# One hybrid block on one core: the end of a chunk taken in single pieces, one per tile, and another order around the tiles

## The chip, the cores and the metric

The kernel runs on one core of one Trainium2 chip. TensorE is called PE here (its weight loads PEld), VectorE DVE, ScalarE ACT, GpSimd POOL, SyncE SP. The metric is the device time of one execution in microseconds (us). A multiplication on PE shows as MATMUL rows; a float32 matmul shows as two rows.

## The reference, cut to what matters

Two sequences of 2048 tokens with 256 features go through four residual parts, each behind a layer norm:

```python
x = x + attn_a(layernorm(x))   # softmax attention, 16 heads, 4 key/value heads
x = x + ffn(layernorm(x))      # three cycles of: tf = sigmoid(net(out)); out = out + coupling * twist(out)
x = x + attn_b(layernorm(x))   # linear attention, causal, no softmax:
#   q, k = rope(silu(y@Wq)), rope(silu(y@Wk)); v = y@Wv
#   out = tril(q k^T) v;  out = layernorm(out * sigmoid(y@Wg1@Wg2)) * ln_w + ln_b;  out @ Wo
x = x + ffn(layernorm(x))      # the same coupling net again
```

## The kernel before, in words

The 4096 tokens lie as 8 chunks of 512 tokens (`NCH`), or 32 tiles of 128 tokens (`TILES`), four tiles to a chunk. `X` holds the residual stream by token, `YT` the normed and transposed stream that the matmuls read. Every engine has its own instruction stream, written out by hand; engines wait for each other by counting semaphores. There are four stages in time: softmax attention, first feed-forward (`feed_forward(0)`), linear attention in tiles (`through_tiles`), second feed-forward (`feed_forward(1)`).

**The tiles.** `through_tiles` calls each engine's `pipeline(n, ...)` for n = 0 to 33. In step n PE computes, in this order: `energy` of tile n (scores, L973), `rows` of tile n-1 (transpose back, L1008), `project_vg` of tile n+1 (L953), `project_qk` of tile n+2 (L944), `turn` of tile n+1 (L961), `attend` of tile n (L987, then L993 once all four masks are there, L999), on some tiles `turn_chunk` (L614), `out_proj` of tile n-2 (L1026), and `norm_turn` of tile n-1 (L1016). DVE computes four masks of tile n (L1734), among them the gated rows of tile n-1 (`gated`, L1755) and their statistics (L1758), then the variance, the rope of tile n+2 (L1718, L1727, L1728), `state` (L1747) and `residual` of tile n-2 (L1773). `project_qk` of tile n+2 writes the PSUM bank that `gated` of tile n-1 reads, so PE holds it until `gated` is done: `wait(pe, l_r, n - 2)`.

**The end of a chunk.** The last cycle of the first feed-forward is not finished before the tiles begin: for chunks 2 to 7 it is done between tiles. For each of these chunks there are seven pieces: `turned_rows` (ACT, L1148), `turned_minus` (DVE, L1599), `joined` (DVE, L1612, writes `X`), `moments_of` (DVE, four statistics L1416 and four aggregates L1423), `root` (POOL, L1838 to L1847), `spread` (ACT, L1140, makes the normed rows), and `turn_chunk` on PE with `put_rows` on ACT (L614, L1071, writes `YT`). On POOL `columns(n)` then copies tile n out of `YT` (L1960) for `project_qk` and `project_vg`. The table `MOMENTS_AT` sets the tile: chunk c has its moments in tile 3c-4, `turned_minus` and `joined` one tile ahead, `spread` one behind, rows two behind.

**The first tail.** The last steps of `feed_forward(0)` (`first`, `second`, `third`, `fourth`, `coupled` on ACT and PE, `update` on DVE) are written out one by one, with the first projections of the tiles among them: `queries_keys` (silu of q and k, L1334), `turned` (L1349 to L1355), `values_gate` (L1342, L1345). Silu and gelu lie in different ACT tables; a change of table is an ACT_TABLE_LOAD.

**The end of the tiles.** For the second feed-forward (stage 3) the moments of chunks 0 to 5 are made in steps 30 to 33, `spread(3, 0)` in step 31, and PE starts `first(0)` of `feed_forward(1)` (L830) once the last `residual` is done.

Of the kernel before, what the change touches and what calls it, by code (L numbers as in the profile page):

```python
# [63 lines left out]
MOMENTS_AT = {-1: 1, **{3 * c - 4: c for c in range(2, NCH)}}  # L64
# [6 lines left out]
def hybrid_block(nc, x, wq, bq, wk, bk, wv, bv, wo, bo, lq, lk, lv, lo, g1, g2, ln_w, ln_b,  # L71
                 c1, d1, c2, d2, c3, d3, c4, d4, e1, f1, e2, f2, e3, f3, ar,
                 ident_in, cos_in, sin_in, causal_in, head_in, diag_in, sign_in, out):
    with ExitStack() as ctx:
# [526 lines left out]
        def _(pe):  # L601
# [179 lines left out]
            def feed_forward(k):  # L781
# [113 lines left out]
                if k == 0:  # L895
# [18 lines left out]
                    project_qk(1, 1)  # L914
# [3 lines left out]
                    pe.wait_ge(n_y, 2 * (2 * NCH + 1))  # L918
                    project_vg(0, 0)
# [109 lines left out]
            def pipeline(n, p, place):  # L1029
# [15 lines left out]
                if n - 2 in MOMENTS_AT:  # L1045
                    turn_chunk(2, MOMENTS_AT[n - 2])
# [4 lines left out]
                if n - 2 in MOMENTS_AT:  # L1051
                    pe.wait_ge(n_y, 2 * (2 * NCH + MOMENTS_AT[n - 2] + 1))

# [12 lines left out]
        def _(act):  # L1066
# [85 lines left out]
            def feed_forward(k):  # L1152
# [71 lines left out]
                for n in range(LAST):  # L1224
# [3 lines left out]
                    if k == 1 and n + 2 < NCH:  # L1228
                        spread(st, n + 2)
# [18 lines left out]
                if k == 0:  # L1248
# [16 lines left out]
                    fourth(LAST - 1)  # L1265
                    first(LAST + 4)
                    second(LAST + 3)
                    coupled(LAST + 5)
                    third(LAST + 1)
                    turned_rows(k, 1)  # L1270
                    second(LAST + 4)
                    fourth(LAST + 1)
                    first(LAST + 5)
                    third(LAST + 3)
                    coupled(LAST + 6)
                    second(LAST + 5)
                    put_rows(2, 0)
                    fourth(LAST + 3)
                    first(LAST + 6)
# [3 lines left out]
                    queries_keys(1, 1)  # L1283
# [3 lines left out]
                    turned(0, 0)  # L1287
                    act.wait_ge(l_vz, 1)
# [77 lines left out]
            def pipeline(n, p, place):  # L1366
# [10 lines left out]
                if n - 2 in MOMENTS_AT:  # L1377
                    put_rows(2, MOMENTS_AT[n - 2])
                if n == TILES - 1:
                    spread(3, 0)  # L1380
                if n == TILES:
                    spread(3, 1)
                    put_rows(3, 0)
                if is_tile(n - 1):
                    affine(n - 1, 1 - p)
                if n - 1 in MOMENTS_AT:
                    spread(2, MOMENTS_AT[n - 1])
                if n + 2 in MOMENTS_AT:
                    turned_rows(0, MOMENTS_AT[n + 2])
                if n == TILES + 1:  # L1390
                    put_rows(3, 1)
# [9 lines left out]
        def _(dve):  # L1401
# [9 lines left out]
            def moments_of(st, c):  # L1411

                g = st * NCH + c
                wait(dve, n_mv, g - 1)
# [621 lines left out]
```

## Time and profile before

| | us |
|---|---|
| median of 3 runs (2078.86 to 2079.82) | 2079.09 |
| the profiled execution, its own time | 2074.16 |
| its span, first to last instruction | 2072.3 |
| PE busy | 1970.2 (95%) |
| DVE busy | 1807.6 (87%) |
| ACT busy | 1493.8 (72%) |
| POOL busy | 199.5 (10%) |

The granted clock of PE is 0.976 of full over the span. A busy share is an average over four stages with different limits; a stage is read by its windows and its timeline. "Idle before, and who ended it" stands in square brackets at the end of a timeline row. Rows of one instruction that follow each other are merged (x4), and the length is from the start of the first to the end of the last.

### The profile page before, as it was taken

To read this page: it belongs to the slowest core of one execution; us is meant where nothing else is said; L and a number is where in the kernel's file an instruction comes from. 1 tells how busy PE (TensorE), PEld (TensorE's weight loads), DVE (VectorE), ACT (ScalarE), POOL (GpSimd) and SP (SyncE) were. 2 spreads that over 40 slices of the span, in tenths; PEclk is the share of its full clock that TensorE was granted. 3 is DMA by queue.
4 is the path that set the end of the run, shared out by engine and by line. 5 is a ranking of instruction groups with operands and counts; after the bars stand their busy time and mean duration, and the time that the engine had idled before them with its cause. 6 is when DMAs were issued, how large, how long until landed. Compare 5 with 4: busy or idle time off the path is not lost.

```text
span 2072.3 us, 47390 instructions
## 1 busy us (share of the span) xinstructions
PE 1970.2 (95%) x14758; PEld 791.0 (38%) x14758; DVE 1807.6 (87%) x3350; ACT 1493.8 (72%) x2955; POOL 199.5 (10%) x442
## 2 busy tenths in 40 slices
PE   7899999999999999999999999989897889998995
PEld 4323333333333333333333333334433555665432
DVE  7899999999999999999999999955447788877358
ACT  5358888888888888888888888855546655545757
POOL 2300000000000000000000000041013111112012
PEclk9879999999999999999999999999999999999998
DMA  5431211221221122122112112122000000000002
GB/s 160 124 101 50 72 55 43 67 62 43 56 72 46 46 71 56 43 65 65 43 51 72 50 44 70 49 92 88 1 1 1 2 2 2 2 2 2 1 1 82
DMA packets 110205, 101.25 MB, mean 49 GB/s; under 512 B 52240, under 2 KB 91424, under 8 KB 110096
## 3 DMA queue, kind: packets, MB, share of 16 engines
q1 hardware_dynamic: 110096, 99.92, 17.7%
q8 instruction: 53, 0.87, 0.2%
q14 instruction: 56, 0.46, 0.1%
HBM read 78.79 MB, written 20.77 MB: 48 GB/s over the span
## 4 chain that ended last, share of the span: by engine, by line
PE 85%; DVE 8%; ACT 4%; issue 2%; DMA 1%; POOL 0%; SPq 0%; ACTq 0%; DVEq 0%; POOLq 0%
PE ps L694 24%; PE ps L669 16%; PE ps L717 11%; PE ps L723 11%; PE ps L830 5%; PE ps L839 3%; PE ps L944 3%; PE ps L953 2%; PE ps L683 2%; PE ps L1026 1%; PE ps L635 1%; PE ps L614 1%; PE ps L993 1%; DVE mx L1514 1%; PE ps L973 1%
## 5 line engine op out<-in xcount | busy, mean ns | idle before, releaser
L1514 DVE TENSOR_REDUCE mx<-ps 128x1 f32<-128x512 f32 x2048 | 1272.8, 682 | 10.8 <-PE ps L669 5.5
L1123 ACT ACTIVATE YT<-ps 128x512 f32<-128x512 f32 x2048 | 1056.5, 603 | 254.6 <-PE ps L723 254.6
L694 PE MATMUL ps<-YT,work 128*32 128x512 f32 x4096 | 546.1, 605 | 0.0
L669 PE MATMUL ps<-work 64*128 64x512 bf16 x2048 | 455.3, 389 | 6.3 <-DVE mx L1514 5.0
L717 PE MATMUL ps<-work 64*128 64x512 bf16 x2048 | 394.7, 378 | 0.1
L723 PE MATMUL ps<-work 34*128 34x512 bf16 x2048 | 393.8, 378 | 0.0
L669 PEld LDWEIGHTS ps<-work 64*128 64x128 bf16 x2048 | 144.7, 93 | 610.6 <-DVE mx L1514 537.1
L717 PEld LDWEIGHTS ps<-work 64*128 64x128 bf16 x2048 | 143.3, 94 | 84.0 <-ACT YT L1123 16.8
L723 PEld LDWEIGHTS ps<-work 34*128 34x128 bf16 x2048 | 100.5, 94 | 77.4 <-issue 1.1
L694 PEld LDWEIGHTS ps<-YT,work 128*32 128x32 f32 x4096 | 80.7, 108 | 120.3 <-ACT YT L1123 112.8
L839 PE MATMUL ps<-work,c_s 128*128 128x512 f32 x192 | 97.5, 633 | 14.9 <-ACT work L1190 9.7
L1734 DVE TENSOR_TENSOR work<-ps,causal 128x512 f32<-128x512 f32 x128 | 81.6, 679 | 14.9 <-PE ps L973 14.7
L1887 POOL TENSOR_TENSOR negq<-mxq,minus 128x16 bf16<-128x16 f32 x32 | 6.9, 216 | 876.5 <-DVE mxq L1503 876.5
L944 PE MATMUL ps<-lqk_s,work 128*128 128x512 f32 x128 | 63.7, 621 | 19.8 <-DVE work L1755 14.4
L830 PE MATMUL ps<-YT,c_s 128*128 128x512 f32 x128 | 60.5, 616 | 5.0 <-ACT vals L1185 2.8
L839 PEld LDWEIGHTS ps<-work,c_s 128*128 128x128 f32 x192 | 36.6, 199 | 69.2 <-issue 49.5
L953 PE MATMUL ps<-lvg_s,work 128*128 128x512 f32 x128 | 61.5, 604 | 0.0
L830 PE MATMUL ps<-YT,ct_s 128*128 128x512 f32 x128 | 60.8, 619 | 0.0
L1342 ACT ACTIVATE work<-ps 128x128 f32<-128x128 f32 x64 | 14.1, 273 | 59.0 <-PE ps L953 59.0
L1878 POOL COPY work<-vals 128x512 f32 (+1 forms) x32 | 19.4, 609 | 330.6 <-PE ps L694 330.5
L1718 DVE TENSOR_TENSOR work<-work,cos_s 128x256 f32<-128x256 f32 x64 | 26.9, 420 | 27.2 <-ACT work L1334 27.2
L1181 ACT ACTIVATE work<-vals,bias 128x512 f32<-128x512 f32 x32 | 21.3, 714 | 39.3 <-DVE vals L1635 39.3
(186 smaller groups left out, 1815.1 us busy)
## 6 DMA issues: line engine op xcount, KB each, us to landing
work<-k_scr SPq DMA_DIRECT2D x640, 64.0 KB, 2.1
work<-q_scr SPq DMA_DIRECT2D x640, 32.0 KB, 1.7
o_scr<-o_sb SPq DMA_DIRECT2D x32, 256.0 KB, 2.1
X<-in_L_attn_a_x_dram SPq DMA_DIRECT2D x8, 512.0 KB, 6.9
work<-negt SPq DMA_DIRECT2D x256, 1.0 KB
work<-o_scr SPq DMA_DIRECT2D x16, 256.0 KB
work<-inv_scr SPq DMA_DIRECT2D x16, 256.0 KB
out_dram<-X SPq DMA_DIRECT2D x8, 512.0 KB, 2.9
```

Of the source, the lines that this page charges most:

```text
L669: mm(ps[:, bank_of[x], :], qa[rows, p, jp, qt * P:(qt + 1) * P], ka[rows, p, kc_ * CH:(kc_ + 1) * CH], start=True, stop=True).then_inc(a_m ...
L683: m = mm(ps[:, last_bank(c, h), (t % 2) * DIM:(t % 2 + 1) * DIM], a_in[:, c % 2, kt, t * P:(t + 1) * P], wo_s[:, kt, :], start=kt == 0, st ...
L694: m = mm(ps[32 * j:32 * j + 32, 7, :], vst[:, p, t, :], prob(GROUP * t + j), start=t == 0, stop=t == KTILES - 1)
L717: mm(ps[:, S_BANK + (u + g) % S_RING, :], kb[rows, p, t * P:(t + 1) * P], qb[rows, p, jp, :], start=True, stop=False)
L723: mm(ps[:, S_BANK + (u + g) % S_RING, :], kc[rows, p, t * P:(t + 1) * P], qc[rows, p, jp, :], start=False, stop=True).then_inc(qk_mm, 1)
L830: m = mm(ps[:, b_ + mt, :], w[:, kt, mt * P:(mt + 1) * P], YT[:, kt, ch(c)], start=kt == 0, stop=kt == KT - 1)
L839: m = mm(ps[:, 2, :], c2_s[:, kt, :], h1[:, n % 2, kt, :], start=kt == 0, stop=kt == KT - 1)
L944: m = mm(ps[:, 0, :], y_st8[:, p, kt, :], lqk_s[:, kt, :], start=kt == 0, stop=kt == KT - 1)
L953: m = mm(ps[:, 1, :], y_st8[:, p, kt, :], lvg_s[:, kt, :], start=kt == 0, stop=kt == KT - 1)
L1123: fn(prob(u), ps[:, S_BANK + u % S_RING, :], ACT.Exp, scale=HD ** -0.5).then_inc(exp_ok, 1)
L1514: dve.tensor_reduce(mx[:, p, at_:at_ + 1], ps[:, bank_of[x], :], AX_X, ALU.max).then_inc(a_max, 1)
L1734: dve.tensor_tensor(e_m[:, i], ps[:, 3 + i, :].rearrange("p (a n) -> p a n", n=P), causal[:].rearrange("p (a n) -> p a n", a=1).broadcast_ ...
```

## The change

It moves instructions and adds none; two table loads of ACT fall away. There are five parts:

1. In the tiles, the end of a chunk goes in single pieces: `turned_minus`, `joined`, the statistics and the aggregates stand in four tiles that follow each other, for chunks 3 to 7 every four tiles (4c-8 to 4c-5); `spread` is in tile 4c-4 and the rows are in tile 4c-3. Chunk 2 is taken in tiles 1 to 5. So the rows of chunk c are there one tile ahead of their use, where they were further ahead.
2. `gated` of tile n-1 stands behind the first mask of tile n, no longer behind the second; its statistics stand behind the second mask.
3. The moments of the second feed-forward for chunks 0 to 4 are made in tiles 24 to 28, chunk 5 in step 33; `spread(3, 0)` is in step 30, `spread(3, 1)` in step 31, `spread(3, 2)` in step 33; both first `turn_chunk(3, ...)` stand in step 32.
4. In the first tail ACT does both last `coupled` at once, DVE both last `update` at once ahead of `turned_minus(k, 1)`, `put_rows(2, 0)` stands behind `fourth(LAST + 3)`, and `queries_keys(1, 1)` behind `turned(0, 0)`; PE does `project_vg(0, 0)` where `project_qk(1, 1)` stood.
5. POOL copies tiles 0 and 1 (`columns`) ahead of `root(2, 1)`.

```diff
-MOMENTS_AT = {-1: 1, **{3 * c - 4: c for c in range(2, NCH)}}
+ENDS = range(3, NCH)
+TURNED_AT = {1: 2, **{4 * c - 9: c for c in ENDS}}
+MINUS_AT = {1: 2, **{4 * c - 8: c for c in ENDS}}
+JOINED_AT = {2: 2, **{4 * c - 7: c for c in ENDS}}
+STATS_AT = {3: 2, **{4 * c - 6: c for c in ENDS}}
+MOMENTS_AT = {3: 2, **{4 * c - 5: c for c in ENDS}}
+SPREAD_AT = {0: 1, 4: 2, **{4 * c - 4: c for c in ENDS}}
+ROWS_AT = {1: 1, 5: 2, **{4 * c - 3: c for c in ENDS}}
+AGAIN_AT = {24 + c: c for c in range(5)}
...
 # PE, first tail
                     project_qk(0, 0)
                     second(LAST + 6)
-                    project_qk(1, 1)
+                    pe.wait_ge(n_y, 2 * (2 * NCH + 1))
+                    project_vg(0, 0)
                     third(LAST + 5)
                     fourth(LAST + 5)
                     turn(0, 0)
-                    pe.wait_ge(n_y, 2 * (2 * NCH + 1))
-                    project_vg(0, 0)
+                    project_qk(1, 1)
...
 # PE, pipeline
-                if n >= TILES:
+                if n == TILES:
                     pe.wait_ge(l_em, 4 * TILES)
-                    turn_chunk(3, n - TILES)
+                    turn_chunk(3, 0)
+                    turn_chunk(3, 1)
...
 # DVE, first tail
                     update(LAST + 5)
+                    update(LAST + 6)
+                    scaled(2, 0)
                     turned_minus(k, 1)
-                    scaled(2, 0)
                     joined(k, 1)
-                    update(LAST + 6)
                     moments_of(2, 1)
...
 # DVE, pipeline
                 if is_tile(n):
                     mask(n, 0)
+                if is_tile(n - 1):
+                    gated(n - 1, 1 - p)
+                if is_tile(n):
                     mask(n, 1)
                 if is_tile(n - 1):
-                    gated(n - 1, 1 - p)
+                    gated_stats(n - 1, 1 - p)
...
-                if n + 1 in MOMENTS_AT:
-                    turned_minus(0, MOMENTS_AT[n + 1])
-                    joined(0, MOMENTS_AT[n + 1])
+                if n in MINUS_AT:
+                    turned_minus(0, MINUS_AT[n])
+                if n in JOINED_AT:
+                    joined(0, JOINED_AT[n])
+                if n in STATS_AT:
+                    stats_of(2, STATS_AT[n])
                 if n in MOMENTS_AT:
-                    moments_of(2, MOMENTS_AT[n])
-                if n >= TILES - 2:
-                    for c in ((0,), (1,), (2, 3), (4, 5))[n - TILES + 2]:
-                        dve.wait_ge(l_x, 4 * (c + 1))
-                        moments_of(3, c)
+                    averages_of(2, MOMENTS_AT[n])
+                if n in AGAIN_AT:
+                    dve.wait_ge(l_x, 4 * (AGAIN_AT[n] + 1))
+                    moments_of(3, AGAIN_AT[n])
...
 # POOL
+            columns(0, 0)
+            columns(1, 1)
             root(2, 1)
-            for n in range(3):
-                columns(n, n % 2)
+            columns(2, 0)
```

Three places of the instruction streams show it. First DVE at the end of a tile, where a chunk's end meets the masks (`qkf_b` holds the turned rows; `ps,causal` is a mask, `work,ps` the gated rows, `stats` their statistics). Before:

```order
L1773 TENSOR_TENSOR X<-X,ps 128x256
L1599 TENSOR_SCALAR qkf_b<-X,end 128x2x64 x4
L1612 SCALAR_TENSOR_TENSOR X<-X,end,qkf_b 128x256 x4
L1734 TENSOR_TENSOR work<-ps,causal 128x512 x2
L1755 SCALAR_TENSOR_TENSOR work<-work,ps 128x256
L1758 BN_STATS stats<-work 128x6
L1734 TENSOR_TENSOR work<-ps,causal 128x512 x2
```

After the change (the tile that takes `joined`):

```order
L1792 TENSOR_TENSOR X<-X,ps 128x256
L1629 SCALAR_TENSOR_TENSOR X<-X,end,qkf_b 128x256 x4
L1751 TENSOR_TENSOR work<-ps,causal 128x512
L1772 SCALAR_TENSOR_TENSOR work<-work,ps 128x256
L1751 TENSOR_TENSOR work<-ps,causal 128x512
L1777 BN_STATS stats<-work 128x6
L1751 TENSOR_TENSOR work<-ps,causal 128x512 x2
```

Of eight instructions between the residual and the first mask four are left, and one mask stands ahead of the gated rows where two stood.

Second ACT in the first tail, from the first silu on (`z_end<-ps` is the last `fourth`, `work<-ps 128x512` the silu, `work<-ps,bias` a gelu). Before:

```order
L1334 ACT_TABLE_LOAD
L1334 ACTIVATE work<-ps 128x512
L1190 ACT_TABLE_LOAD
L1190 ACTIVATE work<-ps,bias 128x512
L1334 ACT_TABLE_LOAD
L1334 ACTIVATE work<-ps 128x512
L1195 ACT_TABLE_LOAD
L1195 ACTIVATE work<-ps,bias 128x512
L1201 ACTIVATE z_end<-ps,half_b 128x8
L1349 COPY work<-ps 128x256
L1352 ACTIVATE work<-ps,parity 128x256 x2
L1355 COPY work<-ps 128x256
```

After the change:

```order
L1343 ACT_TABLE_LOAD
L1343 ACTIVATE work<-ps 128x512
L1199 ACT_TABLE_LOAD
L1199 ACTIVATE work<-ps,bias 128x512
L1204 ACTIVATE work<-ps,bias 128x512
L1210 ACTIVATE z_end<-ps,half_b 128x8
L1358 COPY work<-ps 128x256
L1361 ACTIVATE work<-ps,parity 128x256 x2
L1364 COPY work<-ps 128x256
L1343 ACT_TABLE_LOAD
L1343 ACTIVATE work<-ps 128x512
```

The second silu moved behind the copies of `turned`, and one table load between two gelus went with it; the load ahead of the third silu, further down in tile 0, is gone too.

Third POOL at the same place (`affine` is the last of `token_parts`, `var` and `norm` are `root(2, 1)`, the COPY is `columns`). Before:

```order
L1952 TENSOR_TENSOR affine<-own,turn 128x2x4
L1838 TENSOR_TENSOR var<-moments,eps 128x4
L1840 TENSOR_TENSOR norm<-moments,minus 128x4
L1843 TENSOR_TENSOR norm<-var,mhalf 128x4
L1847 TENSOR_TENSOR norm<-norm 128x4
L1960 COPY work<-YT 128x256 x4
```

After the change:

```order
L1979 TENSOR_TENSOR affine<-own,turn 128x2x4
L1987 COPY work<-YT 128x256 x2
L1865 TENSOR_TENSOR var<-moments,eps 128x4
L1867 TENSOR_TENSOR norm<-moments,minus 128x4
L1870 TENSOR_TENSOR norm<-var,mhalf 128x4
L1874 TENSOR_TENSOR norm<-norm 128x4
L1987 COPY work<-YT 128x256 x2
```

Two of the copies moved ahead of the four instructions of the root.

## Rows read from the trace of the kernel before

**Rows 1.** Windows: length, busy us of PE, PEld, DVE, ACT, POOL, then granted clock.

```profile
1624.77:1803.16 178.39, 163.46 (x1954) 104.71 (x1954) 152.80 (x437) 101.22 (x273) 27.86 (x62) 1.00 0.01 2
1803.16:1877.19 74.03, 74.03 (x902) 47.16 (x901) 59.58 (x162) 33.85 (x99) 7.99 (x18) 1.00 0.01 2
1877.19:1911.00 33.81, 25.71 (x297) 18.02 (x295) 24.91 (x81) 16.79 (x42) 8.18 (x20) 0.90 0.01 2
```

**Rows 2.** Timeline of DVE, an undisturbed tile: start, length, instruction, idle before.

```profile
1844.29 1.29 DVE L1734 TENSOR_TENSOR work<-ps,causal 128x512 f32<-128x512 f32 x2 [0.69 <-PE ps L973]
1845.49 0.41 DVE L1755 SCALAR_TENSOR_TENSOR work<-work,ps 128x256 f32<-128x256 f32 x1
...
1848.67 0.42 DVE L1718 TENSOR_TENSOR work<-work,cos_s 128x256 f32<-128x256 f32 x1 [0.84 <-ACT work L1334]
...
1851.41 0.41 DVE L1773 TENSOR_TENSOR X<-X,ps 128x256 f32<-128x256 f32 x1
1852.51 0.69 DVE L1734 TENSOR_TENSOR work<-ps,causal 128x512 f32<-128x512 f32 x1 [0.69 <-PE ps L973]
```

**Rows 3.** Timeline of PE, the same tile.

```profile
1846.07 1.94 PE L944 MATMUL ps<-lqk_s,work 128*128 128x512 f32 x4
...
1848.83 1.06 PE L993 MATMUL ps<-work 128*32 128x128 f32 x32
...
1849.94 1.13 PE L1026 MATMUL ps<-lo_s,work 128*128 128x256 f32 x4
```

**Rows 4.** Timeline of DVE at the end of tile 4.

```profile
1659.92 0.42 DVE L1773 TENSOR_TENSOR X<-X,ps 128x256 f32<-128x256 f32 x1 [0.45 <-PE ps L1026]
1660.26 1.11 DVE L1599 TENSOR_SCALAR qkf_b<-X,end 128x128 f32<-128x128 f32 x4
1661.49 1.67 DVE L1612 SCALAR_TENSOR_TENSOR X<-X,end,qkf_b 128x256 f32<-128x256 f32 x4
1663.19 1.29 DVE L1734 TENSOR_TENSOR work<-ps,causal 128x512 f32<-128x512 f32 x2
```

**Rows 5.** Timeline of PE from the same moment.

```profile
1660.03 1.15 PE L973 MATMUL ps<-work 32*128 32x256 f32 x16
...
1664.96 1.96 PE L944 MATMUL ps<-lqk_s,work 128*128 128x512 f32 x4 [1.69 <-DVE work L1755]
```

**Rows 6.** Timeline of DVE at the end of tile 2.

```profile
1642.35 1.40 DVE L1416 BATCH_NORM_STATS2 bn<-X 128x6 f32<-128x256 f32 x4
1643.78 0.38 DVE L1423 BATCH_NORM_AGGREGATE moments<-bn 128x2 f32<-128x6 f32 x4
1644.08 1.25 DVE L1734 TENSOR_TENSOR work<-ps,causal 128x512 f32<-128x512 f32 x2
```

**Rows 7.** Timeline of ACT, tail of the first feed-forward.

```profile
1594.10 1.06 ACT L1071 COPY YT<-ps 128x512 f32<-128x512 f32 x2
...
1607.64 1.28 ACT L1334 ACT_TABLE_LOAD   x1
...
1610.84 0.69 ACT L1195 ACTIVATE work<-ps,bias 128x512 f32<-128x512 f32 x1
```

**Rows 8.** Timeline of POOL, the same stretch.

```profile
1599.65 0.74 POOL L1960 COPY work<-YT 128x256 f32<-128x256 f32 x2
```

**Rows 9.** Timeline of PE, the same stretch.

```profile
1600.11 3.54 PE L944 MATMUL ps<-lqk_s,work 128*128 128x512 f32 x4 [4.97 <-POOL work L1960]
```

**Rows 10.** Window around it.

```profile
1596.50:1603.20 6.70, 3.10 (x4) 1.51 (x5) 1.50 (x8) 1.18 (x2) 2.54 (x9) 0.50 0.00 1
```

**Rows 11.** Timeline of ACT in tile 4: the copies of a chunk.

```profile
1658.62 1.07 ACT L1071 COPY YT<-ps 128x512 f32<-128x512 f32 x2 [0.30 <-PE ps L614]
```

**Rows 12.** Timeline of PE after the last tiles.

```profile
1896.39 1.57 PE L993 MATMUL ps<-work 128*32 128x128 f32 x32 [3.15 <-DVE work L1734]
...
1905.12 0.44 PE L1016 MATMUL ps<-ident,work 128*128 128x128 f32 x2 [2.59 <-DVE work L1768]
...
1910.92 1.52 PE L830 MATMUL ps<-YT,c_s 128*128 128x512 f32 x3 [0.77 <-issue]
```

More of the change, by code:

```diff
@@ L1044, in pipeline @@
                     attend(n, p, n % TPB == 0)
-                if n - 2 in MOMENTS_AT:
-                    turn_chunk(2, MOMENTS_AT[n - 2])
+                if n in ROWS_AT:
+                    turn_chunk(2, ROWS_AT[n])
                 if is_tile(n - 2):
@@ L1227, in feed_forward @@
                             global_net(n - GLOBAL_AT[b], b)
-                    if k == 1 and n + 2 < NCH:
+                    if k == 1 and 3 <= n + 2 < NCH:
                         spread(st, n + 2)
@@ L1265, in feed_forward @@
                     fourth(LAST - 1)
+                    coupled(LAST + 5)
+                    coupled(LAST + 6)
                     first(LAST + 4)
                     second(LAST + 3)
-                    coupled(LAST + 5)
                     third(LAST + 1)
+                    first(LAST + 5)
+                    second(LAST + 4)
                     turned_rows(k, 1)
-                    second(LAST + 4)
                     fourth(LAST + 1)
-                    first(LAST + 5)
+                    first(LAST + 6)
+                    second(LAST + 5)
                     third(LAST + 3)
-                    coupled(LAST + 6)
-                    second(LAST + 5)
+                    fourth(LAST + 3)
                     put_rows(2, 0)
-                    fourth(LAST + 3)
-                    first(LAST + 6)
                     act.wait_ge(z_st, 16 * NCH)
@@ L1287, in feed_forward @@
                     turned(0, 0)
+                    queries_keys(1, 1)
                     act.wait_ge(l_vz, 1)
@@ L1376, in pipeline @@
                     act.copy(o_t.rearrange("p a b -> p (a b)"), ps[:, 7, 0:DIM]).then_inc(l_oe, 1)
[L1377 to L1380, printed above, removed]
+                if n in ROWS_AT:
+                    put_rows(2, ROWS_AT[n])
                 if n == TILES:
-                    spread(3, 1)
                     put_rows(3, 0)
+                    put_rows(3, 1)
                 if is_tile(n - 1):
                     affine(n - 1, 1 - p)
[L1386 to L1389, printed above, removed]
+                if n in SPREAD_AT:
+                    spread(2, SPREAD_AT[n])
+                if n in TURNED_AT:
+                    turned_rows(0, TURNED_AT[n])
+                if n in (TILES - 2, TILES - 1):
+                    spread(3, n - TILES + 2)
                 if n == TILES + 1:
-                    put_rows(3, 1)
+                    spread(3, 2)
             feed_forward(0)
@@ L1411, in moments_of, with stats_of @@
             def moments_of(st, c):
-                g = st * NCH + c
-                wait(dve, n_mv, g - 1)
+                stats_of(st, c)
+                averages_of(st, c)
+            def stats_of(st, c):
+                wait(dve, n_mv, st * NCH + c - 1)
                 for t in range(4):
@@ L1417, in moments_of, with averages_of @@
                 m.then_inc(n_bn, 1)
+            def averages_of(st, c):
+                g = st * NCH + c
                 dve.wait_ge(n_bn, g + 1)
@@ L1978, in _ @@
                     root(2, MOMENTS_AT[n])
-                for c in {TILES - 3: (0,), TILES - 2: (1,)}.get(n, ()):
-                    root(3, c)
-            for c in range(2, NCH):
+                if n in AGAIN_AT:
+                    root(3, AGAIN_AT[n])
+            for c in range(len(AGAIN_AT), NCH):
                 root(3, c)
```

9 lines of the change are left out of this document (6 added, 3 removed).

## The prediction

> **What bounds the kernel now.** The change touches the tile stage and its two borders, so I read there: first the windows of the stage, then DVE and PE side by side in a tile with no end of a chunk and in tiles with one, then both borders.
>
> The windows cut the stage at the starts of masks: tile 1, tile 20, tile 29, and the start of the second feed-forward [rows 1]. The nine tiles from 20 on have no piece of a chunk. They take 74.03 us, 8.226 each, and PE is busy for all of it. That is the floor here: a tile is PE's own work, back to back, and nothing in the diff makes it less. The nineteen tiles before them take 178.39 us, where 19 x 8.226 = 156.3 would do: 22.1 too much. Part is PE's own `turn_chunk` for chunks 1 to 7. I price it by tile 19, whose mask-to-mask distance I read as 9.06 us with nothing but such a turn in it: 0.84 each, 5.9 for seven. The other 16.2 us are waits.
>
> What waits is seen at the end of tile 4. DVE does `turned_minus` at 1660.26 and `joined` at 1661.49, and the mask of tile 5 starts only at 1663.19 [rows 4], though its scores started at 1660.03 [rows 5]. In the plain tile scores at 1851.22 gave a mask at 1852.51 [rows 2], so it was due at 1661.32 and is 1.87 late. `gated` stands behind two masks and is late by the same, and PE's `project_qk` waits 1.69 us for just that instruction [rows 5]. Tile 2 shows the milder case: statistics and aggregates fill 1642.35 to 1644.08 [rows 6], and the next mask is 0.96 late by its distance to the mask before it, 9.18 us. Tiles 4, 5 and 6 together take 28.3 us where 24.7 are plain work, and that repeats for each chunk.
>
> **How late a mask may be.** In the plain tile DVE sits idle for 0.69 us before the mask [rows 2]; instructions that follow each other overlap by about 0.08, so a piece of up to 0.77 us fits there at no cost. Behind it there is nearly no slack before: `gated` ends at 1845.49 + 0.41 = 1845.90 [rows 2] and PE's `project_qk` starts at 1846.07 [rows 3], with 0.15 to 0.17 for the semaphore. Now `gated` stands behind one mask, not two. Two masks take 1.20 us (1844.29 to 1845.49), so it comes 0.60 earlier and the mask may be 0.60 late without PE seeing it. The next two bounds hold too: `attend` needs the fourth mask by 1848.83 [rows 3], where I put its end at 1847.55, 1.1 of slack behind the semaphore; and DVE idles 0.84 us before the rope, waiting for the silu [rows 2], so a shift up to 0.84 is gone by the end of the same tile and does not add up over tiles.
>
> **Each piece by this count** (length as the next instruction sees it, minus 0.77 = lateness, minus 0.60 = stall of PE):
> - `turned_minus`: 1.11 - 0.07 of overlap = 1.04; 0.27 late; no stall.
> - `joined`: 1661.49 to 1663.19 = 1.70; 0.93 late; 0.33 of stall in tile 2. For chunks 3 to 7 it shares the tile with the rows of the chunk before, where the residual starts 0.11 ahead of the next scores (1659.92, 1660.03) and in the plain tile 0.19 behind them (1851.41, 1851.22). That gives 0.30 more room: 0.03 of stall.
> - statistics alone: 1.32; 0.55 late; none. Aggregates alone: 0.30; none.
> - both together (tile 3, and the five of `AGAIN_AT`): 1.73 [rows 6]; 0.96 late; 0.36 of stall, in tile 25 with its rows 0.05.
>
> Sum over tiles 1 to 28 after the change: 0.33 + 5 x 0.03 + 0.36 + 4 x 0.36 + 0.05 = 2.3. Before it was 16.2, and tiles 20 to 28 nothing. I take 14 us of gain. Bounds: if every piece stalled PE by its full lateness, the waits would be about 13.7 and the gain 2.5; if none stalled, 16.2.
>
> ACT's pieces hide: `spread` is about 2.1 us behind `affine`, `turned_rows` 1.65, now in different tiles; ACT is busy 101 of 178 us [rows 1]. Without that cover `values_gate` would be late by their length. POOL's root moves with the aggregates and is read one tile on, as before.
>
> **The start.** PE stands idle for 4.97 us ahead of the first `project_qk`, waiting for POOL's copy at 1599.65 [rows 8, 9], which stands behind `root(2, 1)` and so behind moments made after the last `update`. Now the copy waits only for the rows. ACT's `put_rows(2, 0)` ran from 1594.10 [rows 7]; the new order puts a `first` (1.33) and a `fourth` (about 1.0, with its matmul) ahead of it: start 1596.4, end 1597.5, copy at 1597.55: 2.1 us earlier. Then the last `third` no longer stands behind the second silu and its table load: load 1.28, silu 0.60, overlaps aside, 2.1 more. Given back: the second silu now stands behind `turned(0, 0)`, and behind it are its rope, three `last_coupling` and the masks of tile 0. I add these from 1607.4, where the last `fourth` matmuls would start: 1.05 + 0.6 (turn) + 1.4 (copies) + 1.28 (load) + 0.60 (silu), so 1612.4; rope to the memset 4.5, masks 2.5, so 1619.4; rest of `attend` 1.1 [rows 3], scores to mask 1.29: the mask of tile 1 at 1622.1 against 1624.77. Gain 2.7. Bounds: 0, if a new gap in PE's stream eats it; 4.4, if the first `project_qk` runs at full clock.
>
> That clock is a place where a rule bears on it. The row shows four matmuls in 3.54 us where the plain tile has 1.94 [rows 9, 3], with a granted clock of 0.50, the 1.2 GHz level, all around [rows 10], after PE had done nothing for 4.97 us. I keep it at half, since PE would still stand idle about 2 us. The Trainium skill, "TensorE: Matmul & The Clock Gate", Part 1, has it that the gate opens and closes by how busy PE lately was; the trace agrees in that the level fell while PE idled. By that rule the shorter gap might keep full clock, 1.7 us more gain. The other place is the table load, 1.28 us [rows 7]. The Trainium skill, "ScalarE: Activation LUTs", Table sets, gives about 2.7 us for one; by it the two loads that fall away would be worth 5.4 and not 2.6. The trace decides.
>
> **The end.** Before, the mask of tile 31 waits for `moments_of(3, 0)`, 0.7 us; PE waits 3.15 for masks; `gated(31)` stands behind `moments_of(3, 1)`, and PE waits 2.59 for the normalised rows [rows 12]. After: the first is gone (0.7). `norm_turn(31)` no longer waits for DVE but for the second `turn_chunk(3, 1)`, which waits for `spread(3, 1)` (2.1 behind `affine(30)`) and the copy of the bank. I follow it: affine done 1899.6, spread 1901.6, copies and turns to 1903.3, `out_proj(30)` 1.0, `norm_turn(31)` at 1904.25 against 1905.12. No turn stands ahead of the last `out_proj` any more: 1905.65, residual by 1907, `first(0)` at 1907.5 to 1908.3, by PE's clock, against 1910.92. Gain 2.6 to 3.4; I take 3.0. DVE then leads in the second feed-forward, whose first steps are PE's; nothing more comes of it.
>
> **Sum.** 14 + 2.7 + 3.0 = 19.7. The profiled execution took 2074.16 (span 2072.3), so 2054.4 for one like it. The median lies 4.9 above it; I carry that over: 2079.1 - 19.7 = 2059.4.
>
> **The rivals.**
> - *The pieces stall PE anyway.* A late mask also delays the fourth mask and the variance, and DVE is busy 6.6 of 8.2 us in a plain tile (59.58 over nine) [rows 1]. With full lateness the gain is 2.5 + 5.7: 2071. For it: the milder tile 2 passed its whole 0.96 on. Against: the 0.60 is a shift of `gated` itself, which alone held PE.
> - *The tiles gain and the borders don't*: a clock at half in more places, or `turn_chunk(3, 1)` holding PE longer. 14 to 15: 2065.
> - *More than that*: full clock at both borders, no stall in tiles: 16 + 4.4 + 3.4 = 24: 2055.
> - *The rows come too late: slower.* Copies of chunk c end one tile ahead of use: at 1659.69 in such a tile [rows 11], and `project_qk` of the next needs them 3.1 us behind its scores at 1660.03, so at 1663.1. With POOL's copy and a semaphore 2.7 us remain. PE waits only beyond that. To turn 19.7 around over five chunks it must be 4 us more each, 6.7 late; a tile late (8.2) costs 5.5 x 5 = 27, minus 19.7: 2087. For it: nothing between stands in POOL's queue but a root of under 2 us.
>
> **Chances.** The forecast 0.68 (its own range 2056.5 to 2063), stalls anyway 0.10, borders without gain 0.10, more 0.06, too late 0.03, no change at all 0.03 (a part I missed that gives it back). The range takes in forecast and borders and reaches halfway to the first rival: 2054.5 to 2067.5, a little over 8 in 10. A difference under 0.2% (4 us) is not told from none by a measurement of this kernel: faster 0.94, same 0.03, slower 0.03.
>
> **What would show it.** Nine plain tiles at 8.2 us as before; a piece of a chunk in four tiles, each 8.2 to 8.6 and 9.1 with the rows; no wait of PE for `gated` over 0.4 us, the longest in tiles 3 and 24 to 28; POOL's first copy near 1597.5; three table loads in the first tail. Wrong would be: PE's wait for L1772 (`gated`) in most tiles, PE waiting for POOL's copy in tile 10, 14 or 18, or a border longer than before.

## The result, and the profile after

The changed kernel takes 2057.77 us (median of 4 runs, 2057.49 to 2059.16) against 2078.98 for the kernel before on the same chip (2075.68 to 2079.82): ratio 0.9905, 95% interval 0.9893 to 0.9917. That ratio is worth 19.7 us, its interval 17.3 to 22.2; the two medians alone differ by 21.2, which lies inside it. The profiled execution took 2059.16 us, span 2057.3. The forecast was 2059.4.

Windows of the changed kernel, cut at the masks of tiles 1, 20 and 29 and at the second feed-forward (columns as in [rows 1]; the cut at tile 20 lies at that tile's mask):

```profile
1626.75:1787.87 161.12, 160.12 (x1938) 103.69 (x1937) 146.79 (x421) 93.78 (x260) 25.99 (x54) 1.00 0.01 2
1787.87:1865.73 77.86, 77.19 (x921) 49.51 (x920) 71.79 (x218) 41.15 (x115) 20.23 (x42) 1.00 0.01 2
1865.73:1894.27 28.54, 21.77 (x293) 15.26 (x292) 18.11 (x51) 16.82 (x42) 4.32 (x8) 1.00 0.01 2
```

Tiles 1 to 19 take 161.12 us where they took 178.39, and PE is busy for nearly all of it (160.12). Tiles 20 to 28 take 77.86 where they took 74.03 [rows 1], since they now hold chunk 7 and the five moments of the next stage. Together 238.98, which is 13.4 less. The last window is 28.54 where its twin of before is 33.73 (mask of tile 29 to the first matmul of the second feed-forward), and its clock is 1.00 where it was 0.90.

The waits of PE in that stage of the changed kernel (total us, times, longest):

```profile
PE ps L952 <- DVE work L1772: 0.7, 2, 0.4
```

For the kernel before the same view gives 14.4 us in 12 waits, the longest 2.0. But this view shows only what it can tell as a wait. DVE at the end of tile 26, then PE, in the changed kernel:

```profile
1848.34 0.38 DVE L1440 BATCH_NORM_AGGREGATE moments<-bn 128x2 f32<-128x6 f32 x4
1848.64 0.66 DVE L1751 TENSOR_TENSOR work<-ps,causal 128x512 f32<-128x512 f32 x1
1849.21 0.41 DVE L1772 SCALAR_TENSOR_TENSOR work<-work,ps 128x256 f32<-128x256 f32 x1
...
1852.39 0.42 DVE L1735 TENSOR_TENSOR work<-work,cos_s 128x256 f32<-128x256 f32 x1 [0.37 <-ACT work L1343]
```

```profile
1847.74 1.88 PE L961 MATMUL ps<-lvg_s,work 128*128 128x512 f32 x4
1849.77 1.95 PE L952 MATMUL ps<-lqk_s,work 128*128 128x512 f32 x4
1851.56 0.60 PE L969 MATMUL ps<-ident,work 128*128 128x128 f32 x4
```

`project_vg` (L961) starts at 1847.74 and `project_qk` (L952) 2.03 later; with `gated` further ahead the distance is 1.72 in such a tile (below). `gated` ends at 1849.62, 0.15 ahead of L952. The tile takes 8.55 us and a plain one 8.17 (tiles 24 and 26 to 28 of the run `late_again` below, which have no piece): 0.38 lost, 0.31 of it between these two, though no wait is printed. The chain that ended last does show it:

```profile
1848.72 0.57 DVE work L1751
1849.29 0.34 DVE work L1772
...
1849.77 1.95 PE ps L952 x4
```

The first tail, PE, ACT and POOL:

```profile
1590.40 1.96 PE L847 MATMUL ps<-work,c_s 128*128 128x512 f32 x4 [1.39 <-ACT work L1199]
1592.20 0.95 PE L866 MATMUL ps<-w_s,work 128*128 128x2 f32 x8
1594.92 1.71 PE L856 MATMUL ps<-work,c_s 128*64 128x512 f32 x4 [1.77 <-ACT z_end L1210]
1596.55 3.00 PE L847 MATMUL ps<-work,c_s 128*128 128x512 f32 x4
1599.40 1.04 PE L622 MATMUL ps<-ident,xn 128*128 128x128 f32 x8
1600.91 1.05 PE L866 MATMUL ps<-w_s,work 128*128 128x2 f32 x8 [0.48 <-ACT work L1204]
1603.75 1.98 PE L952 MATMUL ps<-lqk_s,work 128*128 128x512 f32 x4 [1.78 <-POOL work L1987]
```

```profile
1592.98 1.64 ACT L1157 ACTIVATE qkf_b<-X,end 128x128 f32<-128x128 f32 x4
1594.52 0.25 ACT L1210 ACTIVATE z_end<-ps,half_b 128x8 f32<-128x8 f32 x1
1594.67 1.33 ACT L1190 ACTIVATE work<-part_b,bias 128x512 f32<-128x512 f32 x2
1599.60 0.69 ACT L1199 ACTIVATE work<-ps,bias 128x512 f32<-128x512 f32 x1 [3.60 <-PE ps L847]
1600.18 0.68 ACT L1204 ACTIVATE work<-ps,bias 128x512 f32<-128x512 f32 x1
1602.01 0.27 ACT L1210 ACTIVATE z_end<-ps,half_b 128x8 f32<-128x8 f32 x1 [1.14 <-PE ps L866]
1602.17 1.06 ACT L1080 COPY YT<-ps 128x512 f32<-128x512 f32 x2
1605.82 1.28 ACT L1343 ACT_TABLE_LOAD   x1 [2.58 <-PE ps L952]
```

```profile
1603.30 0.74 POOL L1987 COPY work<-YT 128x256 f32<-128x256 f32 x2 [6.81 <-ACT YT L1080]
```

PE's `fourth(LAST + 1)` in the kernel before, and the window of the changed one in which `second` runs:

```profile
1588.61 0.95 PE L858 MATMUL ps<-w_s,work 128*128 128x2 f32 x8
```

```profile
1595.20:1598.60 3.40, 3.40 (x7) 1.02 (x4) 3.33 (x12) 0.80 (x2) 1.28 (x4) 0.51 0.02 5
```

This trace runs 2.13 us behind that of before when the coupling of the first feed-forward starts (in the fourteen traces below that start scatters from 1485.2 to 1488.6), in the attention part, which the change doesn't touch. In that count POOL's copy is at 1601.2, later than the 1599.65 of before [rows 8] and not 2.1 earlier. The delay comes in three steps. PE's `fourth(LAST + 1)` (L866) is at 1592.20, 1.46 later in that count than the 1588.61 of before, since the `second` ahead of it waits 1.39 for a gelu of ACT (L1199) that in the new order stands behind both `coupled`; its twin of before has no wait. Then PE waits 1.77 for a z that ACT makes behind `turned_rows` (L1157). And then `second` (L847) takes 3.00 where four matmuls at full clock take 1.96; the granted clock of that window is 0.51.

### The profile page after: what moved, and what is told of

It reads as the page before. It is cut to its first block and busy times, and to the rows that moved or that the text cites. A ratio compares the mean times of both kernels' runs of the same rounds, so it can differ in the third digit from the quotient of the medians.

```text
span 2057.3 us, 47388 instructions
## 1 busy us (share of the span) xinstructions
PE 1969.1 (96%) x14758; PEld 790.6 (38%) x14758; DVE 1805.6 (88%) x3350; ACT 1491.4 (72%) x2953; POOL 202.0 (10%) x442
## 5 line engine op out<-in xcount | busy, mean ns | idle before, releaser
L847 PE MATMUL ps<-work,c_s 128*128 128x512 f32 x192 | 100.1, 647 | 16.2 <-ACT work L1199 11.0
L952 PE MATMUL ps<-lqk_s,work 128*128 128x512 f32 x128 | 62.6, 612 | 3.1 <-POOL work L1987 1.8
L847 PEld LDWEIGHTS ps<-work,c_s 128*128 128x128 f32 x192 | 37.2, 202 | 71.7 <-issue 50.1
L961 PE MATMUL ps<-lvg_s,work 128*128 128x512 f32 x128 | 60.3, 593 | 0.4 <-ACT work L1354 0.4
L622 PE MATMUL ps<-ident,xn 128*128 128x128 f32 x256 | 35.7, 283 | 15.2 <-DVE xn L1449 10.3
```

The costliest lines, as they stand in the source:

```text
L622: m = pe.transpose(ps[:, turn_bank(st, c, kt), t * P:(t + 1) * P], xn[:, c % 2, t, kt * P:(kt + 1) * P], ident[:])
L847: m = mm(ps[:, 2, :], c2_s[:, kt, :], h1[:, n % 2, kt, :], start=kt == 0, stop=kt == KT - 1)
L952: m = mm(ps[:, 0, :], y_st8[:, p, kt, :], lqk_s[:, kt, :], start=kt == 0, stop=kt == KT - 1)
L961: m = mm(ps[:, 1, :], y_st8[:, p, kt, :], lvg_s[:, kt, :], start=kt == 0, stop=kt == KT - 1)
```

## The experiments

All times are ratios to the kernel before on the same chip. Their intervals are 0.0009 to 0.0017 to either side (2 to 3.5 us), so smaller things are read from the traces, in three stretches that start behind the attention part and end ahead of the second feed-forward. Both of these scatter: over the fourteen traces the second feed-forward takes 161.1 to 165.1 us, with the half clock in other places each time, and 161.4 and 163.3 in two traces of the kernel before. The table, in us (coupling: first `coupled` of ACT, which is L1225 in the changed kernel and L1216 in the one before; FFN 2: first matmul of the second feed-forward):

```
                 coupling   mask 1     mask 29            timed
                 to mask 1  to mask 29 to FFN 2   sum     ratio
before           139.61     252.42     33.73     425.76
b_again          139.97     252.59     34.04     426.60   0.9998
gated_only       139.49     245.68     33.10     418.27   0.9969
late_gated       139.39     250.83     31.49     421.71   0.9985
tail_only        139.54     252.58     33.42     425.54   0.9993
after            139.46     238.98     28.54     406.98   0.9905
a_again          139.38     238.80     28.54     406.72   0.9901
old_tail         139.66     238.84     28.53     407.03   0.9914
late_again       139.42     236.58     33.35     409.35   0.9920
fourth_first     136.81     239.03     29.70     405.54   0.9900
gated_ahead      140.20     234.99     28.49     403.68   0.9890
both             137.55     234.98     29.64     402.17   0.9884
before_ahead     140.38     239.41     33.07     412.86   0.9933
ahead_old_tail   140.46     234.98     28.48     403.92   0.9896
```

(With `gated` ahead of the masks every mask comes up to 0.7 later within its tile, so the first column is that much longer and a later one shorter.)

**The same kernels again.** No edit.

> The kernel before, unchanged, as a measure of what this comparison can tell and as a second trace of it. The profile of before was 5 us below the median of its runs, and the two profiles differ by 15.0 us where the medians differ by 21.2. If that is scatter of single executions (a half-clock stretch of PE that falls here or there), the ratio is 1.000 within 0.1%, and a second trace shows half-clock stretches at other places of the same instructions. If one of the two kernels had a lasting difference in a stage that nobody changed, the second trace repeats the first to 0.3 us in every stage.

> The kernel after, unchanged: how far the ratio and the stages of one kernel scatter. Expected 2057.8 us, ratio 0.9905 (0.9893 to 0.9917). If the 1.7 us that the second FFN took more in its profile than the kernel before are scatter, this one's second FFN (first FFN matmul of it to the end) takes anything from 161 to 164 us again; if they belong to the change, 163.1 once more. The 28 periods from the mask of tile 1 to that of tile 29 should take 239.0 us again, within 0.2, since they have no change of clock in them.

Measured 2078.44 us, ratio 0.9998 (0.9989 to 1.0007), and 2058.5 us, 0.9901 (0.9886 to 0.9916). The 28 tiles repeat within 0.2 us. The second feed-forward repeats within 0.5 us in the changed kernel and differs by 1.9 in the one before.

**The fold alone** (part 2 in the kernel before):

```diff
                 if is_tile(n):
                     mask(n, 0)
-                    mask(n, 1)
                 if is_tile(n - 1):
                     gated(n - 1, 1 - p)
+                if is_tile(n):
+                    mask(n, 1)
+                if is_tile(n - 1):
+                    gated_stats(n - 1, 1 - p)
```

> Before, with part 2 alone: the gated rows behind the first mask. My theory: PE waits for the gated rows and for nothing else, and the swap gives 0.60 us of room in each of the 12 tiles with a piece of DVE of 0.96 or 1.87 us lateness: 12 x 0.60 = 7.2 us faster, ratio 0.9965. Rival: the place of the gated rows is worth nothing, since the masks themselves are what PE needs: ratio 1.000. Second rival: it is worth more, because it also lets PE run ahead in plain tiles (8.17 instead of 8.22 in the trace after): 8 to 9 us.

Measured 2072.26 us, 0.9969 (0.9958 to 0.9980); the tiles 6.7 less. Tiles with moments fell from 9.18 to 8.78 us and the one behind them from 8.19 to 7.59, that with `turned_minus` and `joined` only from 10.92 to 10.86. Plain tiles fell from 8.22 to 8.17.

**All but the fold** (part 2 undone in the changed kernel, both masks ahead of `gated` again).

> After, with part 2 undone: the pieces spread, the gated rows again behind two masks. My theory: every piece now stalls PE by its full lateness (0.27, 0.55, 0.63 to 0.93, 0.96), 13.7 us in all where the trace after has about 2.5: 11 us slower than the change, about 2069, ratio to before 0.995. Rival: spreading the pieces is enough by itself, and this takes 2058 like the change, ratio 0.990.

Measured 2075.57 us, 0.9985 (0.9976 to 0.9994). The tiles lost 11.85 of their 13.44, as the room theory had it. Yet the kernel is 17.8 slower than after by the medians, not 11: the end is 2.95 longer too, which I had not counted (the rest lies in the stretches that scatter). Most of these 2.95 may be clock: here the granted clock is 0.51 from 1896.8 to 1903.7, in the changed kernel 1.00 throughout its end, and in the run `fourth_first` below 3.4 us of half clock cost 1.16 in this place, so 6.9 would cost some 2.3, as an estimate. Waits of PE in this kernel's tiles:

```profile
PE ps L952 <- DVE work L1772: 10.1, 21, 0.9
```

21 waits of 0.5 on average where the changed kernel has 2. In all 28 tiles this kernel is 1.6 us below the one before, the fold alone 6.7 and both together 13.4. But the 1.6 isn't the worth of cutting, for this kernel also has the five moments of part 3 in tiles 24 to 28. Counted apart (us):

```
              mask 1 to 24   mask 24 to 29
before        211.29         41.13
gated_only    204.86         40.83
late_gated    203.73         47.10
after         194.89         44.09
late_again    194.91         41.66
before_ahead  198.58         40.83
gated_ahead   192.71         42.28
```

(In the kernels with cut pieces the turn of chunk 7, 0.83, stands in tile 25, in the others in tile 19.) With that turn set apart, cutting alone is worth 6.7 us in tiles 1 to 23, the fold alone 6.4 and both together 15.6. The moments cost 5.1 in tiles 24 to 28 without the fold and 2.4 with it. A stall is what is left of a piece after the idle time and the room, so each helps the other, by 2.4 us here. No run has the cutting without both the fold and part 3; the 6.7 and the 5.1 are read from the tiles of this one.

**The first tail alone, and without it** (parts 4 and 5 put into the kernel before, or undone in the changed one, or undone where `gated` stands ahead).

> Before, with parts 4 and 5 alone (first tail and POOL's order). The prediction had 2.7 us for them. The trace after shows 0.15 us from the start of the first feed-forward to the mask of tile 1. If that trace is typical, the ratio is 1.000; if it caught PE's clock at a bad place, 0.9987.

> The kernel after with the first tail's order undone (its last two parts): PE projects V and G late, ScalarE and DVE in the old order, POOL's root ahead of its first copies. Everything from tile 1 on stays as after. The prediction's theory: 2.7 us slower than after, 2060.5 (ratio 0.9918), all of it between the start of FFN 1 and the mask of tile 1. The reading of the two profiles: the first half of the tail loses 1.4 to 1.5 (third piece behind the z of the one before, then half clock), the second gains 2.1 to 1.7, so only 0.2 us slower, ratio 0.9906. The new order put into the kernel before gave 0.9993 (0.9984 to 1.0002), 1.5 us, between the two. If 28 tiles from mask 1 on differ from 239.0, the tail reaches into the tiles, which none of them says.

> The kernel with gated ahead of both masks, and with the first tail's order of before. Third pair for one question: in the profiles the new tail is worth 0.1 to 0.6 us between the coupling and the mask of tile 1, in the times of two pairs 1.5 (0.9993) and 2.7 (0.9914 against 0.9901), none beyond its interval. If the profile is right, this kernel gives the ratio of the one with gated ahead, 0.9890, within 0.0003; if the times are right, 0.9897 to 0.9903, 1.5 to 2.7 us above it.

Measured 2076.99 us, 0.9993 (0.9984 to 1.0002); 2060.64 us, 0.9914 (0.9901 to 0.9928); 2057.95 us, 0.9896 (0.9881 to 0.9911). From the coupling to the mask of tile 1 the new order is worth 0.07, 0.20 and 0.26 us in three pairs of traces, a tenth of my 2.7 at most. By their ratios the same pairs differ by 1.5, 2.7 and 1.2 us, each within what its intervals allow, and the 0.9896 of the third lies between the two answers that its forecast had set apart. All three point the same way, so something beyond the tail may be gained; no stretch of the traces shows where, and it stays open.

**What ate the tail's gain.** One swap on ACT in the changed kernel:

```diff
                     second(LAST + 4)
-                    turned_rows(k, 1)
                     fourth(LAST + 1)
+                    turned_rows(k, 1)
```

> The kernel after with one swap on ScalarE in the first tail: the fourth piece of the unit LAST+1 (whose z the third FFN piece of LAST+3 on PE waits for) stands ahead of turned_rows, not behind its 1.64 us. Theory from the profile after: z_end comes 1.6 us earlier, at about 1592.9 in its times, PE's third piece starts at about 1593.2 and not 1594.92, put_rows of unit 2, POOL's copy and the first project_qk follow 1.5 us earlier, or up to 3.6 if the two pieces behind it also run ahead of the half clock: 2054.2 to 2056.3 us, ratio 0.9889 to 0.9898. Rival: turned_rows, now 0.3 us later, holds turned_minus and so POOL's copies, and PE waits for these: no gain, 2057.8. Second rival: PE works the same and the half clock falls on the same stretch of work, so that less than 1 us is left.

Measured 2056.53 us, 0.9900 (0.9885 to 0.9915). PE in this kernel, and then two windows:

```profile
1590.62 0.95 PE L866 MATMUL ps<-w_s,work 128*128 128x2 f32 x8
1592.02 1.08 PE L856 MATMUL ps<-work,c_s 128*64 128x512 f32 x4 [0.45 <-ACT z_end L1210]
1593.03 1.98 PE L847 MATMUL ps<-work,c_s 128*128 128x512 f32 x4
1594.85 1.04 PE L622 MATMUL ps<-ident,xn 128*128 128x128 f32 x8
1596.37 1.05 PE L866 MATMUL ps<-w_s,work 128*128 128x2 f32 x8 [0.48 <-ACT work L1204]
1599.21 2.58 PE L952 MATMUL ps<-lqk_s,work 128*128 128x512 f32 x4 [1.78 <-POOL work L1987]
```

```profile
1876.09:1890.56 14.47, 9.28 (x100) 7.29 (x98) 6.24 (x17) 8.79 (x20) 1.08 (x2) 0.88 0.01 2
1880.40:1883.80 3.40, 3.40 (x24) 2.91 (x13) 1.01 (x3) 1.21 (x4) 0.00 (x0) 0.51 0.00 0
```

The wait for z is 0.45 and not 1.77, `second` is at full clock (1.98 and not 3.00), and `project_qk` starts 113.46 us behind the coupling, 3.00 earlier. To the mask of tile 1 that is 2.65 less than after and 2.80 less than before, against a forecast of 2.7. Part of it is clock: in the first tail, from 1590 on, there is one stretch of 3.4 us at half (from 1600.5), where the changed kernel has two (from 1595.2 and from 1612.3). Behind tile 31, where the changed kernel has a clock of 1.00, 3.4 us are at half (the second window), and that gives back 1.16: 14.47 against 13.31 from the mask of tile 31 to the last residual. Net 1.4 by the sums. The times can't tell this from none.

**The last stage's moments late again** (part 3 undone in the changed kernel).

> The kernel after with part 3 undone: moments, spreads and put_rows of the last stage back behind the last tiles, the fold of the gated rows and the tail as after. Theory: tiles 24, 26, 27, 28 lose their pieces and run at 8.17 (1.2 to 1.6 us less over 28 tiles, 237.5), mask 29 to 31 takes 15.7 again (1.2 more), mask 31 to the last residual 16.6 again as with the fold alone (3.3 more): 3 us slower in all, 2060.8, ratio 0.9919. Rival, the prediction's own figure: the pieces ahead of the end gave 3.0 and cost 1.4, so 1.6 slower, 2059.4. Other rival: the 3.3 us behind mask 31 were the clock's alone, which stays full with the fold; then it is about 1 us slower or none.

Measured 2061.62 us, 0.9920 (0.9907 to 0.9934). The end of this kernel on PE:

```profile
1880.94 1.94 PE L1001 MATMUL ps<-work 128*32 128x128 f32 x32 [3.03 <-DVE work L1750]
...
1889.57 0.44 PE L1024 MATMUL ps<-ident,work 128*128 128x128 f32 x2 [2.20 <-DVE work L1786]
1891.21 1.94 PE L622 MATMUL ps<-ident,xn 128*128 128x128 f32 x8 [1.21 <-ACT YT L1079]
1892.95 1.68 PE L1034 MATMUL ps<-lo_s,work 128*128 128x256 f32 x4
1895.40 1.10 PE L838 MATMUL ps<-YT,c_s 128*128 128x512 f32 x2 [0.77 <-issue]
```

And of the changed kernel:

```profile
1883.42 1.08 PE L1001 MATMUL ps<-work 128*32 128x128 f32 x32 [2.40 <-DVE work L1751]
...
1889.32 1.06 PE L622 MATMUL ps<-ident,xn 128*128 128x128 f32 x8 [2.32 <-ACT YT L1080]
...
1891.09 0.38 PE L1024 MATMUL ps<-ident,work 128*128 128x128 f32 x2
1892.37 1.13 PE L1034 MATMUL ps<-lo_s,work 128*128 128x256 f32 x4 [0.90 <-ACT work L1371]
1894.27 1.95 PE L838 MATMUL ps<-YT,c_s 128*128 128x512 f32 x4 [0.77 <-issue]
```

The tiles take 2.4 less, the end 4.8 more. Part of the 4.8 is clock: `turn_chunk` 1.94 for eight where it is 1.04 to 1.06 at full clock, the 32 matmuls of `attend` 1.94 for 1.08. So part 3 is worth 2.4 net by the traces, and by the ratios 3 to 4 within their intervals.

**More room.** `gated` goes one place further, ahead of both masks:

```diff
-                if is_tile(n):
-                    mask(n, 0)
                 if is_tile(n - 1):
                     gated(n - 1, 1 - p)
                 if is_tile(n):
+                    mask(n, 0)
                     mask(n, 1)
```

> The kernel after with gated moved one place further: ahead of both masks of its pair, not between them. Theory (what a piece of a chunk costs is its length less 0.77 of idle and less the room of PE's next project_qk, 0.60 in the kernel after): the room becomes 1.17, all pieces but the first tiles' fit, and of the 4.4 us by which tiles 1 to 28 (238.98) lie above 28 plain ones at 8.17 and seven turns at 0.83 (234.6), 3.5 to 4 go. In tiles with statistics and averages (26 to 28) the period falls from 8.55 to 8.2, where DVE's own work is the bound. In plain tiles gated now waits for the rows (PE, L1016) some 0.3, so the masks are 0.7 late, which attend has 1.1 of slack for. Forecast 2054.2, ratio 0.9885, 28 tiles 235.2. Rival: the masks' 0.7 does hold attend, or the later rope holds energy, and every tile is 0.2 to 0.4 longer: 5 to 11 us slower, ratio 0.993 or more. Second rival: nothing changes since the wait of 0.38 in those tiles was another's than gated's: 2057.8.

Measured 2056.01 us, 0.9890 (0.9873 to 0.9906). The 28 tiles take 234.99 us where 235.2 was forecast, and the floor (28 at 8.17, seven turns at 0.83) is 234.6. The time is 1.8 us above its forecast by the medians. DVE and PE of this kernel in a tile with moments and in the next:

```profile
1853.78 0.38 DVE L1440 BATCH_NORM_AGGREGATE moments<-bn 128x2 f32<-128x6 f32 x4
1854.07 0.39 DVE L1772 SCALAR_TENSOR_TENSOR work<-work,ps 128x256 f32<-128x256 f32 x1
1854.38 1.28 DVE L1751 TENSOR_TENSOR work<-ps,causal 128x512 f32<-128x512 f32 x2
```

```profile
1853.15 1.88 PE L961 MATMUL ps<-lvg_s,work 128*128 128x512 f32 x4
1854.87 1.88 PE L952 MATMUL ps<-lqk_s,work 128*128 128x512 f32 x4
```

`project_qk` follows `project_vg` by 1.72 again. The price of the swap is seen on DVE where nothing made it late, since `gated` now waits there for the rows of PE:

```profile
DVE work L1772 <- PE ps L1016: 3.7, 7, 0.7
```

Up to 0.7 us; five of the seven waits stand ahead of the masks of tiles 8, 12, 16, 20 and 24, right behind a tile that has aggregates alone. PE doesn't wait for what stands behind them: tiles 8, 12, 16 and 20 take 8.17, as long as a plain tile without the swap.

**Both swaps.** `fourth` ahead of `turned_rows`, `gated` ahead of the masks.

> The kernel after with both swaps: the fourth FFN piece of LAST+1 ahead of turned_rows on ScalarE, and gated ahead of both masks on DVE. If the two add up: 2.8 us in the first tail (coupling to the mask of tile 1: 136.7 where after has 139.4) and 3.7 in the tiles: 2051.4, ratio 0.9871. The half clock at 1880 to 1884 that the first swap's profile had behind tile 31, 1.2 us, may come back or not: if it belongs to where that kernel's tail falls, mask 31 to the last residual is 14.5 again, if it is scatter, 13.3. Rival: masks that come late by gated's wait cost in tiles what the tail gains: 2055 to 2060.

Measured 2054.14 us (2053.02 to 2055.86), 0.9884 (0.9868 to 0.9901), span 2051.2. The swaps add up: 4.8 us by the sums, 1.4 and 3.3 alone. The time is 2.7 us above its forecast. The half clock came back 4.0 us behind the mask of tile 31, where the first swap alone had it 4.3 behind; that is two traces of two kernels with the swap against five without it, which speaks against scatter and doesn't rule it out. It is the fastest version here; in time it is 3.6 us under the changed kernel by the medians, by ratios whose intervals overlap.

**Room without cutting.** The kernel before, its pieces left together, with `gated` ahead of both masks and its statistics behind the second (as in the last two).

> The kernel before with one thing changed: gated stands ahead of both masks of its pair, so ahead of the whole first half, with its statistics where the fold of the kernel after has them. Pieces of chunks stay together as before (turned_minus and joined in one tile, 2.8 us). Theory of the room: the fold alone (room 0.60) took 6.8 us from tiles 1 to 28 and left 1.89 us of stall in each chunk's three tiles; room 1.17 leaves about 0.7 in each, so 239 us for the 28 tiles, as much as the whole change reached by cutting the pieces up, and 2065 us in all (ratio 0.9933). Rival: a piece of 2.8 us makes the rest of DVE's tile late too (masks for attend, the rope for energy), and the room at project_qk is no longer what counts: then it stays near the fold's 245.7 us, 2072 us, ratio 0.9967.

Measured 2064.58 us, 0.9933 (0.9919 to 0.9946), and 239.41 us for the 28 tiles; both as forecast. One moved instruction gives in the 28 tiles what the whole change gave (238.98). But the change pays 2.4 us there for part 3, whose gain lies in the end, 28.54 against 33.07 here. In tiles 1 to 23, where the chunks' ends lie, cutting still counts with the full room: `gated_ahead` is 5.0 us below this kernel there, the turn of chunk 7 set apart. Its waits of PE:

```profile
PE ps L944 <- DVE work L1755: 3.0, 6, 0.8
```

Six of 0.5 on average, one for each of the six long pieces, where the kernel before waits 14.4. In the plain tiles 20 to 28 `gated` waits 0.77 or 0.78 us for the rows, and each takes 8.17.

## Why the prediction was right, and where it wasn't

The sum was 19.7 us. From the coupling to the second feed-forward the traces give 18.8, and 19.3 as a mean over the two of each kernel; the timed ratio is worth 19.7, the medians 21.2. It is made up of other parts than I had. The two profiled executions differ by only 15.0, since the changed kernel's lost 2.1 in the attention part and 1.7 in the second feed-forward.

- **The tiles**: forecast 14, measured 13.4 and 13.8. Right, and by its mechanism: stall = length - idle of DVE - room of `project_qk`. Room 0 leaves 11.9 more, room 1.17 leaves 0.4 over the floor. Mis-sized were its terms. The stalls after the change are 4.4 us over the floor, not 2.3: the moments in tiles 24 to 28 hold 1.8 (forecast 1.49) and leave the mask of tile 29 another 0.6 late, each chunk's four tiles hold 0.27 (forecast 0.03), the first seven tiles 0.9 (forecast 0.69). Against that stands a gain that I had ruled out, "nothing in the diff makes it less": the plain tile fell from 8.226 to 8.17, 1.6 over 28, and it does so with the fold alone. So the floor wasn't only PE's own work; that `project_qk` had a little of `gated` in it fits, and no row shows it apart. (The terms of full lateness add up to 13.9, not 13.7.)
- **The start**: forecast 2.7, measured 0.15 (0.6 in the second pair of traces). The step that failed is "the new order puts a `first` (1.33) and a `fourth` (about 1.0, with its matmul) ahead of it: start 1596.4". I counted ACT's queue and left out what PE needs for the matmuls of that `fourth`: they stand behind a `third` that waits for the z of `fourth(LAST + 1)`, and that one is behind the 1.64 us of `turned_rows`. PE idles 1.77, the granted clock is 0.51 right behind that, and `put_rows` starts at 1602.17, 1600.0 in the times of before. The swap shows it: with that order alone mended the stretch gives 2.8. It isn't the whole of the error, though: with the swap the copy of POOL is at 1598.2 in the times of before, so 1.5 earlier and not 2.1, for the wait behind the two `coupled` stays (1.40). The second half of the step was right: tile 0 takes 4.91 from mask to mask where it took 7.05, and three table loads are left in the tail; a change of table costs ACT no more than the load's 1.28 and 0.03 of gaps. The half clock that I kept for the first `project_qk` was wrong: 1.98 us for its four matmuls, full clock, which gave back 1.6 of the 3.6 that POOL's copy was late against its forecast. And the sum has a slip: its terms give 1619.4 + 1.1 + 1.29 = 1621.8 and a gain of 3.0, not 1622.1 and 2.7.
- **The end**: forecast 3.0 (2.6 to 3.4), measured 5.2. The order of events is as told: `attend` waits 2.40 (3.15 before), the second `turn_chunk` is what PE waits for next (2.32), no turn stands ahead of the last `out_proj`. What I left to "PE's clock" is the difference: before, two stretches of 3.4 us here ran at half (from 1896.8 and from 1907.1), after none, and one such stretch costs 1.16 in this place (the first swap). 3.0 + 2 x 1.16 = 5.3. That is an estimate; no run has the end of before at full clock.
- **The second feed-forward**: forecast nothing; the profile has 1.7 more. Two traces of the kernel before differ by 1.9, so this is taken for scatter; traces with the old end take 161.1 to 164.5 here, those with the new one 162.6 to 165.1, and a small lasting loss isn't ruled out.
- **The rivals.** "The pieces stall anyway" held in the kernel without the fold (250.83), not here: the 0.60 was real. Of "the borders don't" half came: the start gave nearly nothing, the end more than forecast. "Too late" didn't come: PE has no wait for POOL's copies in the tiles.

That the total came out within 2 us is in part luck: an error of 2.5 too much at the start and one of 2.2 too little at the end cancel, and the second is the clock's.

## What to carry to other kernels

Work that comes now and then on an engine in order costs its length, less the idle time ahead of it, less the distance between the instruction that the critical engine waits for and the place where it must be. Look for that instruction and move it ahead of what can be late, even if it waits there itself, before cutting the work into pieces: here one moved instruction gave 13.0 us in the tiles, and cutting on top of it 5.0 more. When an order is changed on one engine, follow each operand of the other engine's instructions that now come in between, also the old ones.

## What the runs showed of the hardware

- The same instructions came with one clock in five traces (of four kernels) and with another in two. From the mask of tile 29 to that of tile 31 the changed kernel and the first swap's take 14.49 us each; behind it the one stays at full clock (13.31 us; its repeat and the three others with that end do too, 12.97 to 13.31) and the other has 3.4 us at half (14.47; the kernel with both swaps too, 14.12). What differs is the tail ahead of the stage, and with it the moment at which the stage starts: the mask of tile 1 comes 2.65 us earlier behind the coupling. The pair with `gated` ahead shows it too: 14.78 us in both up to the mask of tile 31, then 12.98 without the swap and 14.12 with it. The Trainium skill, "TensorE: Matmul & The Clock Gate", Part 1, has it that what watches the array runs on by itself and doesn't start with the kernel, so that the point at which the level changes depends on where work falls in it; the traces agree with it, and no run here tests it apart. For a reader it means that a microsecond gained early may be given back by the clock later: here 1.16 of 2.65.
- A stall can be missing from the list of waits. In tiles 26 to 28 of the changed kernel PE lost 0.38 us each with no wait printed; distances between starts in neighbouring tiles show it, and so does the chain that ended last.
